# Attention layers of a two-block transformer kernel: the products of the maxima move from first to third place in every beat of TensorE

## What is computed

```
h = layernorm(x) * (1 + ca) + sa                      # ca, sa, ga: per sequence, from a small input c
q, k, v = projections of h, split into 16 heads of 8
block 0: scores = q k / sqrt(8), causal mask
block 1: scores = q k / sqrt(8) + slope[head] * min(s - t, 0)   # no mask
x = x + ga * (softmax(scores) v) Wo
...
block 0: x = x + gb * (top-2 of 8 experts + a shared expert)(layernorm(x) ...)
block 1: x = x + gb * spikes(relu(h Wfc)^2 Wproj) / 5
```

## Time and profile before

| | |
|---|---|
| median of 3 runs | 1073.48 us (1072.3 to 1075.61) |
| the profiled execution | 1077.53 us, span of its instructions 1075.8 us |
| TensorE busy | 951.1 us (88%) |
| VectorE (DVE) busy | 784.7 us (73%) |
| ScalarE (ACT) busy | 755.6 us (70%) |
| GpSimd (POOL) busy | 539.2 us (50%) |
| mean granted clock of TensorE | 0.966 |
| exponentials, L757 | 832 x 598 ns, idle before them 94.6 us |
| maxima of layer 1, L826 | 256 x 1217 ns, idle before them 39.8 us |

### The profile page before, as it was taken

One profiled execution on the slowest core, in us unless ns is written; L12 is line 12 of the kernel. 1 busy time (PEld: TensorE's weight loads), 2 busy tenths in 40 slices (PEclk: granted clock), 3 DMA queues, 4 the chain that ended last, 5 costly groups with the idle time before them and its releaser, 6 DMA issues. The chain is left out here.

```text
span 1075.8 us, 23037 instructions
## 1 busy us (share of the span) xinstructions
PE 951.1 (88%) x8688; PEld 519.9 (48%) x8688; DVE 784.7 (73%) x1321; ACT 755.6 (70%) x1380; POOL 539.2 (50%) x751
## 2 busy tenths in 40 slices
PE   5688898889898999999999889989899998899896
PEld 3233343334344888888888623333333333333564
DVE  2567777778793766776766589888898988896465
ACT  2367777777776666666666459888888888888663
POOL 4446655675553011101130557786867778665344
PEclk9589999999999999999999979999999999999999
DMA  6432212211301533321343320203112020200011
GB/s 187 155 127 76 57 41 78 72 42 54 84 13 53 130 108 110 91 85 49 102 109 99 93 78 19 74 12 83 31 54 62 24 73 13 82 2 25 23 30 50
DMA packets 61246, 73.91 MB, mean 69 GB/s; under 512 B 14088, under 2 KB 43400, under 8 KB 60624
## 3 DMA queue, kind: packets, MB, share of 16 engines
q1 hardware_dynamic: 61136, 72.44, 24.0%
HBM read 39.24 MB, written 2.77 MB: 39 GB/s over the span
## 5 line engine op out<-in xcount | busy, mean ns | idle before, releaser
L757 ACT ACTIVATE at_E<-at_Sb 128x512 f32<-128x512 f32 x832 | 446.4, 598 | 94.6 <-PE at_Sb L606 88.9
L826 DVE TENSOR_REDUCE at_mx<-at_Mb 128x2 f32<-128x1024 f32 x256 | 297.2, 1217 | 39.8 <-PE at_Mb L569 38.7
L654 PE MATMUL at_Ob<-at_E,VP 128*32 128x256 f32 (+2 forms) x2816 | 215.0, 379 | 13.0 <-ACT Oev L785 7.3
L606 PE MATMUL at_Sb<-QP,KP 64*128 64x512 bf16 (+3 forms) x1024 | 202.6, 346 | 13.4 <-ACT full_k L364 3.6
L569 PE MATMUL at_Mb<-KP,QP 62*128 62x512 bf16 (+3 forms) x1024 | 181.5, 361 | 31.1 <-DVE at_mx L826 28.2
L935 POOL TENSOR_TENSOR at_E<-at_E,at_factor 128x512 f32<-128x512 f32 x128 | 162.4, 1272 | 79.7 <-ACT at_E L757 69.7
L829 DVE TENSOR_REDUCE at_mx<-at_Mb 128x2 f32<-128x768 f32 (+1 forms) x128 | 138.2, 1087 | 72.3 <-PE at_Mb L569 71.1
L946 POOL TENSOR_SCALAR_AFFINE_SELECT at_E<-at_E 128x512 f32<-128x512 f32 x128 | 82.7, 659 | 83.2 <-ACT at_E L757 83.2
L569 PEld LDWEIGHTS at_Mb<-KP,QP 62*128 62x128 bf16 x1024 | 55.0, 97 | 125.9 <-DVE at_mx L826 73.4
L654 PEld LDWEIGHTS at_Ob<-at_E,VP 128*32 128x32 f32 x2816 | 57.0, 108 | 115.2 <-issue 86.0
L606 PEld LDWEIGHTS at_Sb<-QP,KP 64*128 64x128 bf16 x1024 | 74.8, 96 | 74.1 <-ACT at_E L757 34.9
(11 more groups left out here) (185 smaller groups left out, 1428.3 us busy)
## 6 DMA issues: line engine op xcount, KB each, us to landing
QP<-q SPq DMA_DIRECT2D x96, 128.0 KB, 2.4
KP<-k SPq DMA_DIRECT2D x96, 128.0 KB, 2.4
ex_R<-rw_dram SPq DMA_DIRECT2D x32, 256.0 KB, 4.2
ctxN<-Oev SPq DMA_DIRECT2D x16, 256.0 KB, 2.9
denB<-rdram SPq DMA_DIRECT2D x64, 64.0 KB
ex_R<-rw_dram SPq DMA_DIRECT2D x16, 224.0 KB, 4.5
ex_R<-rw_dram SPq DMA_DIRECT2D x16, 192.0 KB, 3.6
ex_R<-rw_dram SPq DMA_DIRECT2D x16, 160.0 KB, 3.4
```

Source lines behind the costliest of these rows:

```text
L606: return pe.matmul(out[:, at:at + SEQ - q0], KP[p0:p0 + ROWS_H, b % 2, 2 * g + a, kt * P:(kt + 1) * P], QP[p0:p0 + ROWS_H, b % 2, 2 * g + ...
L654: last = pe.matmul(Ob[VW * i:VW * (i + 1), 0, q0:q1], weights_of(b, G, kt, i, q0), moving, start=(kt == 0 and q0 == 0), stop=False, skip_g ...
L757: nc.scalar.activation(dst, src, ACT.Exp).then_inc(s["s_read"], 1)
L826: v.tensor_reduce(mx[:, G % 2, :, t % 2, t // 2], src, AX.X, ALU.max).then_inc(s["m_read"], 1)
```

## The change

In each beat the block that calls `max_score` moves behind the loops that call `key_score` and `values`; it stays ahead of the fills and of the output projection. The other engines' queues are as they were, and so is every instruction, buffer and count.

```
             for beat in range(-LEAD, END):
-                if m_of(beat) is not None:
-                    max_score(*m_of(beat))
                 for _, G, t, c in slots_S(beat):
                     key_score(G, t, c)
                 for G, off in zip(*chunks(beat)):
                     values(G, off)
+                if m_of(beat) is not None:
+                    max_score(*m_of(beat))
                 for name in fills(beat):
```

## The result

| | before | after |
|---|---|---|
| median, 4 runs each | 1074.55 us (1072.3 to 1077.78) | 1091.04 us (1090.5 to 1091.56) |
| the profiled execution | 1077.53 us | 1091.51 us |
| span of its instructions | 1075.8 us | 1089.8 us |

The ratio is 1.0144, with a 95% interval of 1.0113 to 1.0175. The kernel became slower by 16.5 us. The forecast, 1079.2 us, had the direction, and the time lies above its range.

What follows compares the result with a forecast made beforehand. It took a chain passing from engine to engine, through POOL in layer 0 and VectorE in layer 1, as the bound. Terms 2.0 + 1.5 + 2.9 - 0.7 = +5.7 us on the 1073.48 median gave 1079.2 us, range 1070 to 1085.

Steps and rivals of the forecast that it cites:

- Step 1: TensorE, a fill now behind M: starts 0.32 us later (at least 0.24), including 0.13 for the change of form.
- Step 2: Layer 0: q later, M saved at T, VectorE's run later; 0.34 us a batch, 2.0 over 6 passes (-1.2 to +3.6).
- The run of VectorE: Layer 0, R of beats 7 to 12: late M, partly offset by later need, costs 0.25 us (0 to 0.4).
- Step 3: Layer 1, full batches: 1.5 us for four passes plus 2.9 for two where the reciprocal doesn't wait.
- Long batches: Layer 1 batches whose reciprocal waits for the `den` DMA, which takes up the lateness: +0.37 us each, 1.5 for four.
- Short batches: Layer 1 batches whose reciprocal doesn't wait, so VectorE's run shifts one beat: +1.47 us each, 2.9 for two.
- Step 4: Start of layer 1: first S no longer behind an M that waits for VectorE; gains 0.7 us (0 to 1.1).
- A: Rival, faster: VectorE's lateness no longer reaches ScalarE in layer 1; 1064.9 us, or 1068.7 with fill costs; chance 0.15.
- point of decision: Layer 1: faster rival holds if S of beat 23 starts over 0.6 us nearer R 21's end than 1.42 us.
- B: Rival, no change: order is a ring, moves cancel, existing waits absorb the fills; 1073.8 us, chance 0.33.
- C: Rival, much slower: maxima too late for T, a quarter of 64 groups lose 0.9 us; 1093 us, chance 0.04.

Runs made afterwards that it cites:

- e8: Changed kernel with only the projection of v moved ahead of M: 1083.7 us, ratio 1.0092 to the kernel before.
- e4: Changed kernel with every M issued one beat earlier, VectorE's and POOL's queues moved along, so only fills and output projection stand behind M: 1082.01 us, ratio 1.0062.
- e6: Changed kernel with the attention's fills and the output projection ahead of M, other fills behind: 1075.92 us, ratio 1.0006 to the kernel before.
- e3: Changed kernel with all fills ahead of the late M, output projection still behind it: 1084.75 us, ratio 1.0093 to the kernel before.
- e5: Kernel before with VectorE's reciprocal in layer 1 one beat later: 1070.6 us, ratio 0.9966.
- e12: Kernel before with layer 1's reciprocal one beat later and, in layer 0, M of beat 3 ahead of T of beat 2: 1064.97 us, ratio 0.991.
- e2: Kernel before with the new order in layer 1 alone, layer 0 in the old order: 1084.0 us, ratio 1.0088.

## Why the prediction was right and wrong

The direction and most of the mechanisms were right. What failed are the terms of Steps 2 and 3: the sum multiplied one worked batch by the number of passes, so the batches that differ from it had no term, VectorE's run in layer 0 and k in layer 1 were priced too low, and the clock in the worked batch wasn't read.

**Step 1, a fill behind M.** Right in size. The timeline of TensorE after, layer 1:

```profile
724.01 0.39 PE L569 MATMUL at_Mb<-KP,QP 62*128 62x512 bf16 x2
724.33 1.12 PE L349 MATMUL at_Sb<-hT,columns 128*128 128x512 f32 x2
...
728.19 0.39 PE L569 MATMUL at_Mb<-KP,QP 62*128 62x512 bf16 x2
728.51 0.23 PE L550 MATMUL at_Sb<-idb,at_nmx 128*32 128x128 bf16 x1
```

A fill comes 0.32 us behind M, and T does too. The estimate had taken 0.31 from the row of V behind S. S starts 0.23 us behind M, so the change of form would account for about 0.1 us. The Trainium skill says that a change of the tiling mode drains TensorE (TensorEngine Tiling (Array Packing), Key Properties). The 0.1 us agree with that, but the runs don't separate it from other reasons. ScalarE's wait for q of layer 1 rose from 0.65 us to 0.97:

```profile
725.49 0.69 ACT L363 ACTIVATE q<-at_Sb,columns 128x512 bf16<-128x512 f32 x1 [0.97 <-PE at_Sb L349]
```

The error was in who pays. I let k in layer 1 be hidden behind a bank that ScalarE holds. It wasn't: ScalarE's wait for k rose from 0.15 to 0.55 us, and by beat 28 a batch had lost another 0.4.

**Step 2, layer 0: +2.0 forecast, +6.2 at the end of the layer.** The pattern batch looks right: batches 2 and 3 grew by 0.20 and 0.17 us, where 0.34 was forecast, and T of beat 2 waits less:

```profile
167.93 0.22 PE L550 MATMUL at_Sb<-idb,at_nmx 128*32 128x128 bf16 x1 [1.31 <-POOL at_nmx L918]
```

But this pattern hides two larger numbers. At full clock a batch grew by 1.39 us, as batch 1 shows (36.01 to 37.40), and from batch 2 on the clock gave 1.18 of it back. In batch 1, by the starts of E: -0.32 at the T that waits (forecast -0.23), +0.83 between beats 6 and 12, over VectorE's run (0.25; v behind M is in it, and e8, with v ahead of M, has batches of 37.15 us, 0.25 less), +0.14 behind the transposition of x, +0.43 at q (0.32; ScalarE's wait rose from 0.90 to 1.34 us), and +0.33 behind it that had no term.

Three steps failed. The worked batch has a clock of 0.95, and I read lengths off it as if it were 1.00: that the wait of 1.70 us also cost 1.18 us of clock stood in the row. "The run of VectorE", bounded by 0 and 0.4, was over twice its upper bound. And "for 6 passes from batch to batch" took one batch for all. Batches 4 and 5 have VectorE's weight splitting in them and grew by 1.37 and 1.72 us although the clock gave 1.18 back in each, and e8 takes back 0.96 and 1.45. I never asked what stands behind an M that waits. Batches 0 and 7 added 0.65 and 1.05, less 0.5 because the first S came earlier. The 0.65 are no shown price, since batch 0 varies by more than that between executions of the same layer 0 (38.54 to 39.88 us in the old order, 38.94 to 39.90 in the new one). Batch 7, 29.48 us before and 30.53 after, takes 29.82 with M at its old place and the fills behind it (e4) and 30.16 with M late and the fills ahead (e6).

**Step 3, layer 1: +4.4 forecast, +7.65 measured.** In the full batches the mechanism was found again, term by term. S of beat 23 starts 1.15 us behind the end of R of beat 21, at 718.78 behind an R pair that ended at 716.43 + 1.21 = 717.64 (one R takes 1.21 us):

```profile
716.43 2.34 DVE L826 TENSOR_REDUCE at_mx<-at_Mb 128x2 f32<-128x1024 f32 x2
...
717.69 1.16 PE L288 MATMUL at_Mb<-wog,ctxT 128*128 128x128 f32 x8 [0.96 <-DVE at_mx L826]
718.78 0.39 PE L606 MATMUL at_Sb<-QP,KP 64*128 64x512 bf16 x2
```

The reciprocal waits for `den` in no batch of layer 1 (6.6 us over 6 waits before, in the whole program; after, one of 0.8 at the end).

- Long batches: forecast +0.37 each, 1.5 for four. Measured +0.50, +0.10, +0.42 and -0.59, together +0.4. In batch 5, E of beat 23 comes 0.61 us earlier (forecast 0.27), x and q cost the 0.32 each that was forecast, and k 0.39 that was not.
- Short batches: forecast +1.47 each, 2.9 for two. Measured +2.18 and +2.13, together 4.3. In batch 3, VectorE's run starts 1.28 us later and ends 1.40 later (forecast 1.1), E of beat 23 is 1.14 us late, x and q add 0.64 and k 0.40.
- Batch 0 (+1.81) and batch 7 (+1.10) had no term. That is 2.9 us, almost the whole miss of this step, since the misses of the long and the short batches (-1.1 and +1.4) nearly cancel, by luck. The two have different causes. Batch 7 pays for the late M: it takes 41.28 us in e3 too, where M is late and the fills stand ahead of it, and 40.39 in e4, where M is at its old place. Its reciprocal never waited, so nothing covers the lateness, as in the short ones. Batch 0 pays for what stands behind M: 45.95 us in e3, 47.51 in e4.

**Step 4.** The first S of layer 1 comes 1.1 us nearer to the first M; 0.7 was forecast, with 1.1 as the far end.

**The sum and its base.** The sum is 8.3 us short of what the profiled executions show: 4.2 in layer 0, 3.25 in layer 1 and 1.4 between them, less 0.4 at Step 4 (8.45, within the rounding of the batches' ends). The 1.4 had no term and go with the fall of the clock. Another error lies in how it was put on the median. The term for the wait of `den` came from an execution that had four long batches. The median execution has fewer: e5, which removes them, gains 7.1 us on the profiled span but only 4.25 on the median. Where the base has fewer long batches the change costs more. The sum's own lines said so, +1.47 against +0.37, and the sum was still added to the median as it stood. By 4.25 / 7.1 the median execution would have 2.4 long batches (an estimate), 1.6 short ones more, each 1.1 us dearer: 1.8 us. So the range ended too early above: its bounds covered the size of each term, and not the batches that had none.

**The rivals.** A fell: only batch 6 of layer 1 got shorter (by 0.6 us), and the five from 1 to 5 all take 48.2 us. Its point of decision was never reached: S came 0.27 nearer to R of beat 21, and the run itself came later. B fell with it. C, the only rival slower than the forecast, was near the measured time for the wrong reason: T waits for `nmx` 13.2 us in 11 places after, where it waited 16.3 in 13 before.

```profile
  ACT at_E L757: 26.2, 61
  POOL at_nmx L918: 13.2, 11
```

(The waits of L550 on TensorE after, weight loads included: which engine ended them, us in all, times. The first row grew from 15.7 us, 12 times: T now stands ready behind M and waits for a bank.)

## What to carry to other kernels

Read the granted clock of the very stretch that is to serve as the pattern, before any length is taken from it: here a wait of 1.31 and not 1.70 us went with 1.2 us less lost to the clock. When a waiting step moves within an in-order queue, list what comes to stand behind it and who waits for each item; in the full batches of layer 1 the output projection and the fills behind M cost nearly all, and the lateness of M itself almost nothing. Look at the first and last pass by themselves: the last one paid 1.1 us for the lateness. If one profile shows the same loop body in two lengths, find what picks the length before taking any sum from it: it changes the base, and here it was a gain of its own.

## What was not expected of the hardware

A wait of TensorE for 1.70 us was followed by 3.5 us at half clock in five batches of six, a wait of 1.31 us in the same place by none in six, and one M inside the wait (e12, 1.38 us left) kept the clock up too. In the profiled executions of all these kernels, waits of 1.31 to 1.38 us in this place were never followed by a fall (54 places in nine kernels), those of 1.70 us in 15 of 18 places with the old order of layer 0 (before, e2, e5), and in 3 of 12 where T stands ahead of M (e3, e6). So the length of the wait alone doesn't decide; what else does isn't shown.

The time that SyncE's queue takes to issue six DMAs varied from 3.8 to over 5 us in the same program and the same place (one issue took up to 1.8 us, the median is 0.60). These 0.9 us decided between batches of 46.07 and 47.8 us, in which VectorE, ScalarE and GpSimd ran the same number of instructions (46, 79 and 44). Why an issue takes longer at times isn't shown by any run here.
